# Two attention layers on one core: ScalarE's exponentials and copies moved behind later heads, one sum per head, and one product for the first layer's total

## The reference

```
x = x + _L0_gnn_ref(_layernorm(x, axis=-1), adj, L0_gnn_W, L0_gnn_a)
x = x + _L0_ffn_ref(_layernorm(x, axis=-1), ...)
x = x + _L1_gnn_ref(_layernorm(x, axis=-1), adj, L1_gnn_W, L1_gnn_a)
x = x + _L1_ffn_ref(_layernorm(x, axis=-1), ...)

# first attention (_L0_gnn_ref)
e = jax.nn.relu(f_src[:, :, None] + f_dst[:, None, :])
att = jnp.where(adj > 0, e, NEG)
att = jax.nn.softmax(att, axis=2)
h_prime = jnp.einsum('bnm,bmf->bnf', att, h)

# second attention (_L1_gnn_ref), 8 heads of 16 features
e = e1[:, :, :, None] + e2[:, :, None, :]
e = jnp.where(mask, -jnp.inf, e)
e = jnp.where(e >= 0, e, ALPHA * e)
attn = jax.nn.softmax(e, axis=-1)
h_prime = jnp.einsum('bhij,bhjd->bhid', attn, Wh)
```

## Time and profile before

| | |
|---|---|
| time, median of 3 runs | 1854.22 us (1849.24 to 1857.61) |
| the profiled execution's own time | 1853.88 us |
| its span in the profile | 1852.0 us |
| TensorE's mean granted clock | 0.799 of full |
| busy: TensorE, VectorE, ScalarE, GpSimd | 1189.8, 1109.8, 1026.8, 901.3 us |
| first attention's products (L876) | 145.0 us in 1024 records |
| second attention's products (L1437) | 258.4 us in 4096 records, waits of 162.2 us ahead of them |
| ScalarE's comparisons (L1471) | 403.5 us in 384 records |
| VectorE's mask products (L1329) | 163.4 us in 64 records |

### The profile page before, as it was taken

The page is one execution under the profiler, slowest core; times in us unless marked ns, Lnnn a source line. Parts: engine busy times, 40 slices in busy tenths (PEclk is TensorE's granted clock), DMA queues, the critical chain, the costliest instruction groups (busy, mean ns, idle before and its releaser), DMA issues. The chain is left out here.

```text
span 1852.0 us, 29489 instructions
## 1 busy us (share of the span) xinstructions
PE 1189.8 (64%) x10171; PEld 1021.1 (55%) x10171; DVE 1109.8 (60%) x2506; ACT 1026.8 (55%) x1440; POOL 901.3 (49%) x710
## 2 busy tenths in 40 slices
PE   3788778620867675047767667767666129999870
PEld 2777677620656554035546455555554129999760
DVE  4687876731333332569999888888898214333324
ACT  4576666420544442069797685868684126666530
POOL 1013554675456555021352566576656735665550
PEclk9798888855778786569898787877877559999985
DMA  7643441113544441732221222212211155555518
GB/s 230 234 176 132 145 143 51 44 39 112 155 122 136 115 127 50 203 114 73 79 81 59 69 87 72 96 67 91 84 48 43 45 185 147 168 169 164 155 34 271
DMA packets 166116, 213.59 MB, mean 115 GB/s; under 512 B 29812, under 2 KB 121102, under 8 KB 164944
## 3 DMA queue, kind: packets, MB, share of 16 engines
q1 hardware_dynamic: 147792, 175.99, 30.7%
q0 software_dynamic: 18176, 35.72, 5.5%
HBM read 156.71 MB, written 58.56 MB: 116 GB/s over the span
## 5 line engine op out<-in xcount | busy, mean ns | idle before, releaser
L474 POOL DMA_INDIRECT y_dram<-f_ys,f_Xb x312 | 316.5, 1014 | 265.8 <-DVE f_ys L495 180.9
L1471 ACT ACTIVATE g_near<-g_s_row,g_steep 128x1024 fp8e4<-128x1024 f32 x384 | 403.5, 1138 | 0.1
L185 POOL DMA_INDIRECT xs_dram<-r_row,r_pos x256 | 289.8, 1132 | 184.4 <-issue 77.8
L1437 PE MATMUL g_bp<-g_G,g_near 128*128 128x102 bf16 x4096 | 258.4, 236 | 162.2 <-DVE g_near L1329 153.3
L1437 PEld LDWEIGHTS g_bp<-g_G,g_near 128*128 128x128 fp8e4 x4096 | 247.0, 114 | 186.1 <-issue 185.5
L541 PE MATMUL f_ops<-f_w,f_g 128*128 128x128 f32 x1872 | 275.9, 290 | 45.4 <-issue 26.9
L541 PEld LDWEIGHTS f_ops<-f_w,f_g 128*128 128x128 f32 x1872 | 259.1, 204 | 72.3 <-issue 32.6
L577 ACT ACTIVATE f_g<-f_hps,f_ex 128x512 f32<-128x512 f32 x234 | 158.8, 689 | 195.7 <-PE f_hps L533 111.0
L1329 DVE TENSOR_TENSOR g_near<-g_near,g_mask 128x2048 uint32<-128x2048 uint32 x64 | 163.4, 2553 | 45.1 <-ACT g_near L1471 22.9
L482 DVE TENSOR_TENSOR f_XTl<-f_XTf,f_XTh 128x512 fp32r<-128x512 f32 x78 | 54.1, 693 | 174.7 <-ACT f_XTf L563 107.4
L876 PE MATMUL attout<-V,Pt 128*128 128x129 f32 x1024 | 145.0, 301 | 14.5 <-DVE Pt L729 14.5
(11 more groups left out here) (233 smaller groups left out, 2131.1 us busy)
## 6 DMA issues: line engine op xcount, KB each, us to landing
raw<-in_adj SPq DMA_DIRECT2D x64, 512.0 KB, 6.1
g_s_row<-rows_dram SPq DMA_DIRECT2D x64, 512.0 KB
f_Xb<-xs_dram SPq DMA_DIRECT2D x78, 288.0 KB
f_w<-in_L_ffn_W SPq DMA_DIRECT2D x78, 256.0 KB
f_yb<-y_dram SPq DMA_DIRECT2D x16, 1024.0 KB, 6.2
f_w<-in_L_ffn_W SPq DMA_DIRECT2D x78, 128.0 KB
mask_dram<-mask SPq DMA_DIRECT2D x16, 512.0 KB, 4.0
g_mask<-mask_dram SPq DMA_DIRECT2D x8, 1024.0 KB, 5.3
```

The source lines that it names most:

```text
L185: pool.indirect_dma_start(rows_d, bass.IndirectOffsetOnAxis(ap=pos[:, c % 2, k, t:t + 1], axis=0), row[:, c % RB, k, t, :], None, bounds_c ...
L474: pool.indirect_dma_start(y_d.rearrange("n k d -> (n k) d"), bass.IndirectOffsetOnAxis(ap=Xb[:, i % XB, r, D:D + 1].bitcast(U32), axis=0), ...
L1437: ins = pe.matmul(bp[h % 2][:, t // 4, (t % 4) * 6 * C:(t % 4 + 1) * 6 * C], near[:, k % 3, j, t * P:(t + 1) * P], G[:, s, j, h, :, :], st ...
L1471: ins = act.activation(near[:, k % 3, j, :], s_row[:, k % 3, :], ACT.Relu, scale=STEEP, bias=steep[:, s, j, h:h + 1], saturate=False)
```

## The change

What changes, in the first layer: VectorE sums V over the eight tiles (`vsum`) behind the diagonal, and TensorE makes the total by one product with the ones; `maximum` moves ahead of the router's logits, the total behind the source sums, and ScalarE's copy of the total from behind its masks of tile 7 to ahead of them. In the second: FACTORS moves from place 9 to 13, SCALED from 9 to 10, HIGH from 13 to 15, and MIDDLE behind the comparison of head 0 of the next step; the two sums of Bf of a head become one; the reciprocal `rden` moves from head 2 to head 3, behind the router's placing; and ScalarE's normalisation for the router moves from head 2 to head 3.

```
 def largest(c):
     dve.tensor_scalar(diag[:, :], ident[:, :], dmax[:, 0:1], None, ALU.mult).then_inc(s_dg, 1)
+    wait(dve, s_hs, c)
+    dve.reduce_sum(vsum[:, :], V[:, c % 2, :, 0:D].rearrange("p t d -> p d t"), AX.X).then_inc(s_vs, 1)
...
-                    pe.wait_ge(s_V, c * 3 + 3)
-                    for j in range(NT):
-                        ins = pe.matmul(misc[:, 0:D], ones[:, :], V[:, f, j, 0:D], start=(j == 0), stop=(j == NT - 1))
-                    ins.then_inc(s_hs, 1)
+                    pe.wait_ge(s_vs, c + 1)
+                    pe.wait_ge(s_dM, c + 1)
+                    pe.matmul(misc[:, 0:D], ones[:, :], vsum[:, :], start=True, stop=True).then_inc(s_hs, 1)
...
+                    if prepare and t == 5:
+                        maximum(b + 1)
                     if t == 5 and 0 <= r < B:
                         R.pe_logits(pe, r)
                     if prepare:
                         if t < 5:
                             project(b + 1, 1 - s, t)
-                        elif t == 5:
-                            project(b + 1, 1 - s, 6)
                         elif t == 6:
                             project(b + 1, 1 - s, 5)
+                            project(b + 1, 1 - s, 6)
                         transpose_adj(b + 1, t)
-                    if prepare and t == 5:
-                        maximum(b + 1)
...
-                if prepare:
-                    total(b + 1, 1 - s)
-
+                    if t == 6 and prepare:
+                        total(b + 1, 1 - s)
...
-        0, 4, (6, 8), (11, 13), (0, 2, 4), (3, 5, 7), 7, 8, 9, 9, 13, 15
+        0, 4, (6, 8), (11, 13), (0, 2, 4), (3, 5, 7), 7, 8, 13, 10, 15, 17
...
-                for g in range(2):
-                    dve.reduce_sum(Bf[:, s, 4 * g:4 * g + 4, h, :], bp[h % 2][:, g, 0:4 * 6 * C].rearrange("p (t s c) -> p t c s", s=3, c=2 * C), AX.X).then_inc(s_Bf, 1)
+                dve.reduce_sum(Bf[:, s, :, h, :].rearrange("p (g t) c -> p g t c", g=2),
+                               bp[h % 2][:, :, 0:4 * 6 * C].rearrange("p g (t s c) -> p g t c s", s=3, c=2 * C), AX.X).then_inc(s_Bf, 2)
...
-                    if h == 2 and done:
+                    if h == 3 and done:
                         dve.wait_ge(s_sum, b)
                         dve.reciprocal(rden[:, :, :, :], t1[:, :, :, HD:C]).then_inc(s_rden, 1)
-                    if h == 2 and ends(b):
+                    if h == 3 and ends(b):
                         add(dve, b - 1)
...
                     if work:
                         compare(b, s, h)
+                    if h == 0 and b > 0 and work:
+                        prepare_at(b, s, MIDDLE)
...
-                    if h == 2 and 0 <= r < B:
+                    if h == 3 and 0 <= r < B:
                         R.act_normalise(act, r)
...
+                if b == -1:
+                    prepare_at(0, 0, MIDDLE)
```

More of the change, by code:

```diff
@@ L606, in phase_gat0 @@
     diag = sb("diag", [P, P], FP32)
+    vsum = sb("vsum", [P, D], FP32)
     ndmax = sb("ndmax", [P, 1], FP32)
@@ L645, in phase_gat0 @@
     s_dm, s_dg, s_mx, s_dM, s_nd = sem("g0_dm"), sem("g0_dg"), sem("g0_mx"), sem("g0_dM"), sem("g0_nd")
-    s_hs, s_hsum = sem("g0_hs"), sem("g0_hsum")
+    s_vs, s_hs, s_hsum = sem("g0_vs"), sem("g0_hs"), sem("g0_hsum")
     s_Pt = [sem(f"g0_Pt{i}") for i in range(2)]
```

## The result

| | |
|---|---|
| before, median | 1855.17 us (1849.24 to 1857.61, 4 runs) |
| after, median | 1830.37 us (1826.24 to 1833.7, 4 runs) |
| ratio | 0.987, 95% interval 0.9839 to 0.9901 |
| the profiled execution after | 1830.34 us (span 1828.4) |

What follows compares the result with a forecast made beforehand. The two attention layers hold all gain: a TensorE, ScalarE, VectorE loop bounds the first, VectorE nearly always works in the second. 14 us from each, 28 us off 1853.9, gives 1826 us, range 1812 to 1842.

Steps and rivals of the forecast that it cites:

- the middle of 2.4 us: First layer, TensorE's time saved per step by the one-product total, between 3.2 us and 1.5 us.
- the slow stretch stays: Rival, chance 0.1: TensorE's slow clock falls on later products; first layer gives 7 x 1.1, second 4 us, time 1842.
- the deduction: First layer: 0.4 us a step taken off because the largest value's product, now ahead of the logits, waits for VectorE's diagonal.
- (a): Second layer, steady step, end of head 3's mask product to end of head 5's: 21.7 us, +5.3.
- (b): Second layer, from head 5's mask product to the end of head 0's in the next step: 26.3 us, -4.8.
- (c): Second layer, from head 0's mask product to the router's shift: ended by GpSimd's root, change 0.
- (d): Second layer, router's shift to end of head 3's mask product: the 5.45 us wait for GpSimd's combination goes, -5.9.
- the wait of 4.7 us: Second layer, steady step: new wait of VectorE for ScalarE's factors ahead of the scaling, to cover GpSimd's moved products.
- I add 1 us: Second layer, heads 5 to 0: allowance for GpSimd's work meeting other VectorE operations and TensorE's slower next head.
- a sign that it fails: Second layer: the forecast is wrong if TensorE waits for the low part, forecast hidden by 3.0 us.
- The second layer gives nothing: Rival, chance 0.2: GpSimd's moved products are uncovered, gains only pay for the first steps' 7 us; time 1840.
- The new wait does not come: Rival, chance 0.15: TensorE runs head 3 quicker, ScalarE's lead carries, six steps gain 4.7 us more; time 1798.

Runs made afterwards that it cites:

- the first layer alone: Only the change's first-layer edits, on the kernel before, second layer untouched: 1846.06 us, ratio 0.9957.
- one product in the old order: Kernel before with the total made by one product of V's first tile only, no VectorE sum, order unchanged, output not the reference's: 1828.73 us, ratio 0.9891.
- the reciprocal alone: Kernel before with only the reciprocal and the last step's add moved from head 2 to head 3: 1845.29 us, ratio 0.9968.
- The second layer alone: Only the change's second-layer edits, on the kernel before, first layer untouched: 1838.55 us, ratio 0.991.
- two groups of edits: Reciprocal and last add moved to head 3 on the kernel before, 1845.29 us; kernel after with just these back at head 2, 1858.71 us.
- the best edit of this study: GpSimd's two subtractions for the middle and low parts made by VectorE: 1803.59 us on the kernel after, 1869.75 us on the one before.

## Why the prediction was right, and where it was not

**First layer, forecast 14 us.** The first attention ends at 453 to 455 us in five traces with the old code, and at 440, 441, 441, 445 and 451 in five with the changed one: 10.7 us on average, of which the trace after drew the smallest, 2.8. By time it is 8 us. The term was right in kind and too large. The step that failed is the middle of 2.4 us, taken between 3.2 and the 1.5 us of a slow stretch that stays: with the new order the slow stretch stays, less the deduction 1.1 us a step, 7.7 in all. The case had stood at 0.1. Behind the start of a step's weights, the source sums of the three steady steps end after 37.9 to 39.2 us before, 38.7 to 39.0 after, 36.4 to 37.6 with the first layer alone, and 35.5 to 35.9 with one product in the old order. After, all three have logits of 3.42 us and an attention product of 3.75 behind them; the one product in the old order, 20 us, shows what the removal is worth without these.

The reading behind the deduction was wrong as well: "at most 1.2 us, in other steps nothing". It measured the wait for the diagonal from the start of the logits at 186.59, but these had themselves waited 1.30 us for the router's input. The diagonal is done 27.9 to 28.1 us behind the weights in all these traces, and TensorE waited for it 2.0 to 3.6 us in three steps of each of the six with the new order. What the wait adds is less, since it takes the place of the other: the logits start 28.5 to 28.7 us behind the weights after, and 27.3 to 28.7 before. So the 0.4 us was near by luck.

What the prediction drew from the rule of the Trainium skill ("TensorE: Matmul & The Clock Gate", Part 1), that the slow stretch can stay when products are taken away, came with the new order only: the clock of this stretch was 0.57 and 0.69 there, 0.83 with one product in the old order, and 0.84 before (186 to 197 us). VectorE's sum was longer than bounded (1.98 us against 1.4) and still covered, as forecast. The wait for the copied total shrank, 3.13 to 1.31, and the wait for the weights grew, 1.08 to 3.49, as forecast.

**Second layer, forecast 14 us.** Its own steps gave 12.8. Cut into the prediction's four stretches, the step from 1064.99 on is (a) 20.9 us (forecast 21.7; its start, head 3's mask product, is that of the next step less 80.56), (b) 28.1 (26.3), (c) 13.4 (13.5) and (d) 18.1 (17.2): 80.6 against 78.8, where the three steady steps measured 78.1, 80.6 and 76.1. In (a) the sum was right and its content was not: the wait of 4.7 us was filled by GpSimd's hold on VectorE (3.5) and left 0.8. That is the cover as the prediction described it, seen from the other side. In (b) "I add 1 us" for GpSimd's work meeting other operations is the mis-sized term: it was 2.7 (8.5 less 5.8). In (d) the prediction had no term for the normalisations, which took 0.9 us more. Over the whole layer the first two steps lost 4.5 us instead of 7, the three steady ones gave 14.3 instead of 12.8 and their share of the 3 for the single sum, and the late ones with the tail 3 instead of 5.5. These misses have both signs, so that 12.8 comes so near 14 is partly luck. So is the whole: in the two traces 7.8 us of the 24 lie in the last expert stage. TensorE waited for the low part in two steps, 7.3 us each, which the prediction had named as a sign that it fails (its slack was 3.0 us). The time did not follow: one of the two is the steady step of 76.1 us. The low part was late there because a mask product held GpSimd, which spared VectorE a second hold.

**The rivals.** "The second layer gives nothing" took GpSimd's products as uncovered. That is what happens to the reciprocal alone. Its own sum, 3 x 2.1 + 4.5 = 10.8 against 7, leaves 4 us and so 1836, not 1840. "The new wait does not come" had the right row and the wrong consequence, since what replaced the wait took as long.

**What stays open.** The second layer alone took 14 to 20 us off by time and 12.6 in its own steps; the difference lies within the spread of the expert stage. Why TensorE's clock is higher in one execution than in another of the same code is not settled (that it made the difference of 11 us is argued from five traces, no run sets it), nor which part of the new order (the total's slot, its copy, or the product for the largest value) puts the slow products there: with only the last undone, the first attention ended no sooner.

## What to carry to other kernels

When a wait ends, ask what was held in it. Here VectorE lost 10 us of waits a step and won 3.6, since GpSimd's long two-input operations met its small ones instead of its idle time. Work moved to another engine to relieve a busy one can cost the busy one more than doing it (8.5 against 4.8 us). And an edit tried alone can be judged wrongly: two groups of edits worth +1 and -13 us gave +13 together, and the best edit of this study, worth 23 to 27 us on the changed kernel, cost 18 on the one before.

## What the runs showed of the hardware

An operation of VectorE on 64 elements a partition, 0.22 us by itself, took up to 5.13 us (second layer alone, at 1329.57) beside a subtraction of 2176 elements on GpSimd. Comparisons with one tensor input were held too (3.41 us for two, otherwise 1.41), and so was a scaling of 64 elements (1.72 for 0.20). In the other order, a mask product that had started 0.34 us earlier kept its 2.29 us, and GpSimd's subtraction took 5.85 us for 4.04. The reductions of TensorE's products kept their length beside it (1.06 us at 1182.28, with GpSimd subtracting from 1182.33). The granted clock of one stretch of TensorE's program was 0.57 and 0.69 in two executions of the same code, whose first attentions ended at 451 and 440 us.
